# Selective-scan, expert and attention kernel: last C product of a sequence on VectorE, transposes ahead of the gating, normalisation and first tap on ScalarE

## The reference

```
xn = layernorm(x)
# layer 0, a selective scan with 256 channels and 16 states, beside an expert network
hs, gate = split(xn @ in_proj_w.T)
u   = silu(conv1d(hs, conv_w, 4 taps, pad (1, 2)) + conv_b)
dt, Bm, Cm = rmsnorms of the three parts of u @ x_proj_w.T
dt  = softplus(dt @ dt_proj_w.T + dt_proj_b)
h_t = exp(dt_t * A) * h_(t-1) + (dt_t * u_t) * Bm_t        # along the 512 tokens, for 16 states n
y   = sum over n of h[n] * Cm[n] + u * D
y   = y * silu(gate)
x   = x + y @ out_proj_w.T + expert(xn)                    # one of 8 experts per token
# layer 1
xn  = layernorm(x)
x   = x + attention(xn, 16 heads, window +-32) @ Wo + bo + ffn(xn)
```

## Time and profile before

| | |
|---|---|
| median of three runs | 1202.01 us (1197.09 to 1203.52) |
| the profiled execution: its own time | 1201.24 us |
| its span, first to last instruction | 1199.3 us, mean granted TensorE clock 0.922 of 2.4 GHz |
| busy: PE / DVE / ACT / POOL | 925.0 (77%) / 868.6 (72%) / 590.0 (49%) / 434.5 (36%) us |
| chain that ended last, by engine | PE 34%, DVE 26%, issue 16%, POOL 13%, ACT 7% |
| chain, largest lines | DVE hst L709 11%, PE y_bank L1148 10%, POOL hc L1066 7% |
| VectorE gates the sum (L800) at | 243.56, 380.60, 504.64, 628.59, 752.07, 875.71, 999.30, 1109.64 us |

### The profile page before, as it was taken

The page is one execution under the profiler, slowest core; times in us unless marked ns, Lnnn a source line. Parts: engine busy times, 40 slices in busy tenths (PEclk is TensorE's granted clock), DMA queues, the critical chain, the costliest instruction groups (busy, mean ns, idle before and its releaser), DMA issues.

```text
span 1199.3 us, 14581 instructions
## 1 busy us (share of the span) xinstructions
PE 925.0 (77%) x4474; PEld 589.7 (49%) x4474; DVE 868.6 (72%) x1333; ACT 590.0 (49%) x1362; POOL 434.5 (36%) x234
## 2 busy tenths in 40 slices
PE   3553788856887788778879787978787877888786
PEld 2413676724554454445446454545454544455555
DVE  8673544669778977898679868887888778776242
ACT  2142555624654555554555456445635562654442
POOL 3273221343622362237233623363235423533000
PEclk9566999987998999999999999889988999999998
DMA  8163878942321332133223321332223323520000
GB/s 283 48 200 128 247 240 285 238 104 71 83 63 53 97 85 74 49 105 88 73 55 100 92 76 53 87 89 84 60 73 90 78 57 77 105 81 7 10 1 9
DMA packets 79553, 116.77 MB, mean 97 GB/s; under 512 B 4849, under 2 KB 40049, under 8 KB 79345
## 3 DMA queue, kind: packets, MB, share of 16 engines
q1 hardware_dynamic: 73184, 108.99, 32.5%
q0 software_dynamic: 6288, 6.82, 2.5%
HBM read 103.73 MB, written 12.06 MB: 97 GB/s over the span
## 4 chain that ended last, share of the span: by engine, by line
PE 34%; DVE 26%; issue 16%; POOL 13%; ACT 7%; DMA 2%; DVEq 1%; SPq 0%; POOLq 0%; ACTq 0%
DVE hst L709 11%; PE y_bank L1148 10%; POOL hc L1066 7%; PE more L1237 5%; POOL xs_d L1031 3%; DVE dBu L701 3%; POOL x_res L1047 3%; ACT pexp L980 2%; PE work_l L1229 2%; PE work L1167 2%; PE work_l L1223 2%; DVE nmax L823 1%; ACT pT L985 1%; DMA hst<-in_hidden 1%; PE more L1245 1%
## 5 line engine op out<-in xcount | busy, mean ns | idle before, releaser
L1066 POOL TENSOR_TENSOR hc<-hst,bcr 128x1024 f32<-128x1024 f32 x124 | 304.3, 2454 | 600.6 <-DVE dBu L701 547.6
L1148 PE MATMUL y_bank<-hc,pk 128*128 128x512 f32 x512 | 269.1, 652 | 74.7 <-POOL hc L1066 64.1
L709 DVE TENSOR_TENSOR_SCAN hst<-dA,dBu 128x1024 f32<-128x1024 f32 x128 | 291.7, 2279 | 8.0 <-ACT dA L904 5.8
L1148 PEld LDWEIGHTS y_bank<-hc,pk 128*128 128x128 f32 x512 | 98.6, 204 | 186.7 <-POOL hc L1066 86.0
L904 ACT ACTIVATE dA<-dt,neg_a 128x511 f32<-128x511 f32 x256 | 170.6, 726 | 18.8 <-DVE hst L709 16.3
L701 DVE TENSOR_TENSOR dBu<-dtu,bcr 128x1024 f32<-128x1024 f32 x128 | 159.3, 1245 | 12.7
L1237 PE MATMUL more<-vw,pT 96*128 96x99 f32 x1024 | 129.2, 277 | 35.8 <-ACT pT L985 24.5
L1237 PEld LDWEIGHTS more<-vw,pT 96*128 96x128 f32 x1024 | 119.1, 191 | 68.3 <-DVE fsg L843 31.2
L985 ACT COPY pT<-work 96x512 f32<-96x512 f32 x64 | 37.2, 582 | 154.0 <-PE work L1229 154.0
L823 DVE TENSOR_REDUCE nmax<-work 128x4 f32<-128x384 f32 x64 | 35.5, 554 | 62.6 <-PE work L1223 62.6
L980 ACT ACTIVATE pexp<-work_l,nmax 128x96 f32<-128x96 f32 x256 | 66.0, 341 | 5.8 <-DVE nmax L823 5.0
(11 more groups left out here) (293 smaller groups left out, 1459.8 us busy)
## 6 DMA issues: line engine op xcount, KB each, us to landing
bcr<-bc_d SPq DMA_DIRECT2D x128, 512.0 KB, 4.9
qbd<-in_wx SPq DMA_DIRECT2D x8, 578.0 KB, 4.3
attn<-in_wx SPq DMA_DIRECT2D x8, 578.0 KB, 5.0
pT<-in_wx SPq DMA_DIRECT2D x8, 578.0 KB, 5.4
kT<-in_wx SPq DMA_DIRECT2D x8, 578.0 KB, 5.2
vw<-in_wx SPq DMA_DIRECT2D x8, 578.0 KB, 4.9
xs_d<-rbuf POOLq DMA_DIRECT2D x1, 2560.0 KB, 9.8
hst<-in_hidden SPq DMA_DIRECT2D x8, 256.0 KB, 5.4
```

Source lines behind the costliest of these rows:

```text
L709: v.tensor_tensor_scan(hst[n % 2][:].rearrange("p h t -> p (h t)"), dA[n % 2][:].rearrange("p h t -> p (h t)"), dBu[:].rearrange("p h t -> ...
L1066: g_.tensor_tensor(hc[n % 2][:], hst[n % 2][:], bcr[n % RING][:, 1:2, :].to_broadcast([P, NH, L]), ALU.mult).then_inc(s_hc, 1)
L1148: last = t.matmul(y_bank[h][:], ident, hc[n % 2][:, h, :], start=False, stop=(n == N - 1))
```

## The change

It does four things, all in slots 0 to 4 of a turn and at the end of the scan:

1. The C product of the last state, `hc` of n = 15, moves from GpSimd (L1066) to VectorE, right behind the scan of that state and ahead of `dtu`, the last averages and `dBu` of the next sequence. It now waits on VectorE for the product before it and for the sum that read its buffer.
2. Slot 0 begins with the units of a new list `EDGE`: the last sum, then `attnT` (from slot 2), `xnT` (from the middle of slot 0), then the gating (now a unit of its own, `gated`) and `out`. This moves the transposes on TensorE, their copies on ScalarE (L991, L910) ahead of the decay of state 1, and on SyncE the load that follows `xnT`.
3. `ln_b` leaves VectorE: ScalarE computes `xn1` as rstd * x + shift, with a shift of -mean * rstd for which VectorE issues one more small instruction and GpSimd another.
4. `conv0` leaves VectorE: ScalarE computes one tap (that of weight 1, which needs no neighbour) from `bank0` before it copies the projection out, and VectorE adds the taps 0, 2, 3. `bank0` is thus read twice by ScalarE for each of `hs0` and `hs1`.

The core of the diff:

```diff
@@ plan
-PRE_AT = {0: ["xnT"], 1: ["hs0"], 2: ["hs1"], 3: ["conv0", "zg0"], 4: ["conv1", "sg0"], ...
+PRE_AT = {0: ["xnT"], 1: ["hs0"], 2: ["hs1"], 3: ["zg0"], 4: ["conv1", "sg0"], ...
+EDGE = [("attn", "y_end"), ("finish", "attnT"), ("pre", "xnT"), ("attn", "gated"), ("attn", "out")]
...
         if slot == 0:
-            units.append(("attn", "y_end", 0))
-            units += [("attn", name, 0) for name in LAYER1_AT.get(0, [])]
+            units += [(lane, name, 0) for lane, name in EDGE]
@@ VectorE
+                if n == N - 1:
+                    dve.wait_ge(s_h, b * N + N)
+                    dve.wait_ge(s_hc, b * N + N - 1)
+                    dve.wait_ge(s_ys, b * (N + 1) + N - 1)
+                    v.tensor_tensor(hc[n % 2][:], hst[n % 2][:], bcr[n % RING][:, 1:2, :].to_broadcast([P, NH, L]),
+                                    ALU.mult).then_inc(s_hc, 1)
...
+                tap = (1, 0, 2, 3)[k]
                 for h in range(NH):
-                    if k == 0:
+                    if k == 1:
+                        dve.wait_ge(s_tap, b * NH + h + 1)
                         done0(dve, b, f"hs{h}")
-                        before(dve, s_de, b)
-                        v.tensor_scalar(z[0][:, h, :], src, w, half_c[:, NH * KC + h:NH * KC + h + 1],
-                                        ALU.mult, ALU.add).then_inc(s_conv, 1)
...
-                if name == "y_end":
+                if name == "gated":
...
+                    v.tensor_scalar(shift1[:], mv1[:, :, 0], -1.0, None, ALU.mult).then_inc(s_stat1, 1)
-                elif name == "ln_b":
-                    dve.wait_ge(s_rstd1, b + 1)
-                    for j in range(NT):
-                        v.tensor_scalar(xn1[:, j, :], x1r[par][:, j, :], mv1[:, j, 0:1], rstd1[:, j:j + 1],
-                                        ALU.subtract, ALU.mult).then_inc(s_xn1, 1)
@@ ScalarE
+                    s.activation(z[0][:, h, :], bank0[:], ACT.Identity, bias=half_c[:, NH * KC + h:NH * KC + h + 1],
+                                 scale=half_c[:, h * KC + 1:h * KC + 2]).then_inc(s_tap, 1)
                     s.copy(hs[:, h, 1:1 + L], bank0[:]).then_inc(s_free0, 1)
...
                 if name == "ln_b":
+                    act.wait_ge(s_rstd1, b * 2 + 2)
+                    for j in range(NT):
+                        s.activation(xn1[:, j, :], x1r[par][:, j, :], ACT.Identity, bias=shift1[:, j:j + 1],
+                                     scale=rstd1[:, j:j + 1]).then_inc(s_xn1, 1)
@@ GpSimd
-                if n + 1 < N:
-                    pool.wait_ge(s_dBu, b * N + n + 2)
-                else:
-                    pool.wait_ge(s_h, b * N + n + 1)
+                pool.wait_ge(s_dBu, b * N + n + 2)
...
+                        g_.tensor_tensor(shift1[:], shift1[:], rstd1[:], ALU.mult).then_inc(s_rstd1, 1)
```

More of the change, by code:

```diff
@@ L71 @@
 FFN_AT = {12: 0, 16: 1, 20: 2}
-PRE_AT = {0: ["xnT"], 1: ["hs0"], 2: ["hs1"], 3: ["conv0", "zg0"], 4: ["conv1", "sg0"], 5: ["conv2", "zg1"], 6: ["conv3", "sg1"], 8: ["th1"], 9: ["xdbl"], 10: ["ss"], 12: ["xdr"], 13: ["bc"], 15: ["dtT"], 18: ["dtp0"], 19: ["drl0", "dtp1"], 21: ["drl1"], 22: ["de"], 23: ["dw"], 24: ["dln"], 25: ["dt"], 26: ["dtu"], 27: ["start"], 7: ["th0"]}
+PRE_AT = {0: ["xnT"], 1: ["hs0"], 2: ["hs1"], 3: ["zg0"], 4: ["conv1", "sg0"], 5: ["conv2", "zg1"], 6: ["conv3", "sg1"], 8: ["th1"], 9: ["xdbl"], 10: ["ss"], 12: ["xdr"], 13: ["bc"], 15: ["dtT"], 18: ["dtp0"], 19: ["drl0", "dtp1"], 21: ["drl1"], 22: ["de"], 23: ["dw"], 24: ["dln"], 25: ["dt"], 26: ["dtu"], 27: ["start"], 7: ["th0"]}
 LAYER1_AT = {0: ["out"], 1: ["x1"], 2: ["ln_a"], 3: ["ln_b"], 4: ["q", "k"], 5: ["v0", "v1"], 6: ["v2", "v3"]}
 FINISH_AT = {2: ["attnT"], 3: ["fin"], 4: ["y_out"]}
+EDGE = [("attn", "y_end"), ("finish", "attnT"), ("pre", "xnT"), ("attn", "gated"), ("attn", "out")]
 LAG = {"pre": -1, "scan": 0, "attn": 1, "late": 2, "finish": 2}
@@ L97, in plan @@
         units += [(lane, "scores", g) for lane, g in of("scores", slot)]
-        if n is not None:
+        if n is not None and (slot or ("scan", "step") not in EDGE):
             units.append(("scan", "step", n))
@@ L106, in plan @@
             for name in at.get(slot, []):
-                if slot or lane != "attn":
+                if (lane, name) not in EDGE:
                     units.append((lane, name, 0))
@@ L291, in program @@
         rstd1 = sb("rstd1", [P, NT])
+        shift1 = sb("shift1", [P, NT])
         xn1 = sb("xn1", [P, NT, H])
@@ L376, in program @@
         s_conv = sem("conv_steps")
+        s_tap = sem("first_tap_ready")
         s_tg = sem("gate_tanh_ready")
@@ L719, in step @@
                                     ALU.mult).then_inc(s_hc, 1)
+                if n == N - 1:
[4 more added lines that the diff above has]
+                                    ALU.mult).then_inc(s_hc, 1)
             def conv(k, b):
+                tap = (1, 0, 2, 3)[k]
                 for h in range(NH):
[L724 to L726 removed]
+                    if k == 1:
+                        dve.wait_ge(s_tap, b * NH + h + 1)
                         done0(dve, b, f"hs{h}")
[L728 to L734 removed]
+                    else:
+                        dve.wait_ge(s_conv, b * NH * (KC - 1) + (k - 2) * NH + h + 1)
+                    v.scalar_tensor_tensor(z[k % 2][:, h, :], hs[:, h, tap:tap + L],
+                                           half_c[:, h * KC + tap:h * KC + tap + 1], z[(k - 1) % 2][:, h, :],
+                                           ALU.mult, ALU.add).then_inc(s_conv, 1)
             def pre(name, b, par):
@@ L807, in layer1 @@
                     done1(dve, b, "out")
+                    before(dve, s_xn1, b * NT)
                     for j in range(NT):
                         v.bn_stats(stats1[:, j, :], x1r[par][:, j, :]).then_inc(s_stat1, 1)
-                    dve.wait_ge(s_stat1, b * 9 + 4)
+                    dve.wait_ge(s_stat1, b * 10 + 4)
                     v.memset(tick[:], 0.0)
@@ L913, in pre @@
                     full0(act, b, name)
-                    before(act, s_conv, b * NH * KC)
+                    before(act, s_conv, b * NH * (KC - 1))
+                    s.activation(z[0][:, h, :], bank0[:], ACT.Identity, bias=half_c[:, NH * KC + h:NH * KC + h + 1],
+                                 scale=half_c[:, h * KC + 1:h * KC + 2]).then_inc(s_tap, 1)
                     s.copy(hs[:, h, 1:1 + L], bank0[:]).then_inc(s_free0, 1)
@@ L923, in pre @@
                     take0(act, b, name)
-                    act.wait_ge(s_conv, b * NH * KC + (KC - 1) * NH + h + 1)
+                    act.wait_ge(s_conv, b * NH * (KC - 1) + (KC - 2) * NH + h + 1)
                     s.activation(bank0[:], z[1][:, h, :], ACT.Tanh).then_inc(s_full0, 1)
@@ L1072, in body @@
                         early(name, k)
-                    if name == "step" and not (isinstance(b, int) and b == 0 and k < DVE_C):
+                    if name == "step" and k < N - 1 and not (isinstance(b, int) and b == 0 and k < DVE_C):
                         times_c(b, k)
@@ L1083, in body @@
                     elif name == "ln_a":
-                        pool.wait_ge(s_stat1, b * 9 + 9)
+                        pool.wait_ge(s_stat1, b * 10 + 10)
+                        before(pool, s_xn1, b * NT)
                         g_.tensor_tensor(rstd1[:], var1[:], minus_half[:, 0:NT], ALU.pow).then_inc(s_rstd1, 1)
+                        pool.wait_ge(s_rstd1, b * 2 + 1)
+                        g_.tensor_tensor(shift1[:], shift1[:], rstd1[:], ALU.mult).then_inc(s_rstd1, 1)
             iterations(pool, body)
```

7 lines of the change are left out of this document (1 added, 6 removed).

## The result

The changed kernel took 1187.96 us in the median of seven runs (1186.16 to 1192.08), the kernel before 1202.07 on the same chip: ratio 0.9892, 95% interval 0.987 to 0.9914. The forecast of 1189 was met. The profiled execution took 1187.72 us with a span of 1185.9 us, which is 13.4 us less than before; the forecast's sum was 12.7 us. But the sum came out right from terms of which some were wrong by 1 to 4 us in opposite directions, so the profile is worth more here than the total.

A forecast was written before the change was run, and what follows sets the result against it. Neither VectorE nor TensorE is full; what matters is where both stand still, as at the border between turns. Five full turns x 1.75 = 8.8, plus 1.1, 2.5 and 0.3, together 12.7 us: 1189 us, range 1181 to 1198.

The forecast's parts named there:

- The last C product: Border between turns: with the product on VectorE in 1.22 us, the gating starts 2.1 us earlier (1.9 in the worse case).
- The transposes: TensorE at the border: both kinds take 2.0 us, done before the gated halves are there; any delay of `out` is hidden.
- Cost nothing: Border: the moved transposes run from 501.3 to 503.3, before the gated halves at 503.85, so they add no time.
- half-clock rival: Between `hs0` and `hs1`, emptied of `attnT`: TensorE's clock falls before `fin`, `y_out` slips 4.0 us; 1208 us, chance 0.06.
- The chain to `fin`: Gating to `y_out`: `hs1` starts at 514.6 against 516.00, and `y_out` can start 1.9 us earlier, VectorE idle 3.9 us there.
- Some 20 us in all: Sign in the profile after: VectorE waits 3 to 4 us at `y_out` for `fin` in each full turn, this in total.
- The normalisation and the tap: Before `y_out`: 3.19 + 0.99 us leave VectorE, nothing fills their place; ScalarE's normalising, taken as 1.5 us, is hidden.
- The first gated turn: Wait for the expert rows' DMA eats the border's gain; without `y_out` part of the removed work counts: 1.1 us gained.
- Turn 7 and the end: Turn 7, without next input or `hs0`, gains the whole 2.1 plus some tenths: 2.5 us; turn 8 gains 0.3.
- The rival of a quicker TensorE: Border sum and what follows run at full clock, each turn gaining up to 2.6 us: 1183 us, chance 0.2.

The follow-up runs named there:

- x1_hc_only: The kernel before with only the last C product moved to VectorE; order, normalisation and first tap as before: 1188.36 us, ratio 0.9933.
- x9_old_order: The changed kernel with the transposes of attention and of the next input back in their old place: 1187.47 us, ratio 0.9907 to the kernel before.
- x2: The kernel before with only the normalisation and first tap moved to ScalarE; C product and order as before: 1200.23 us, ratio 1.001.
- x10: The changed kernel with only the attention transposes back between the projections; the input's stay ahead of the gating: 1192.11 us, ratio 0.9953 to the kernel before.

## Why the prediction was right, and where it was not

The five full turns, divided at the starts that the timelines give (us in all; in brackets the difference to before):

| | scan of state 15 to gating | gating to scan of state 3 | scan of state 3 to that of state 15 | all |
|---|---|---|---|---|
| before | 46.6 | 106.9 | 464.8 | 618.25 |
| forecast | (-10.5) | (+1.75) | (0) | (-8.8) |
| changed | 40.3 (-6.3) | 109.6 (+2.8) | 463.5 (-1.3) | 613.42 (-4.8) |
| x1_hc_only | 38.3 (-8.3) | 106.8 (-0.1) | 464.2 (-0.6) | 609.31 (-8.9) |
| x9_old_order | 41.5 (-5.1) | 104.8 (-2.1) | 464.1 (-0.7) | 610.41 (-7.8) |

**The last C product: the mechanism right, the size too large.** It took 1.22 us and the `dBu` behind it 1.23, as forecast. But it gave 6.3 us in the five turns where 5 x 2.1 = 10.5 had been taken, and this is the largest part of what is missing. Measured from the scan of state 15, the gating starts 1.7, 1.5, 2.3 and 0.9 us earlier in turns 2, 3, 5 and 6, and in turn 4 not at all (10.17 us against 10.04). Two things stood in the way. The first is in the rows of the changed kernel around the start of turn 3:

```profile
487.83 1.08 PE L1238 MATMUL work<-pk,pexp 128*96 128x128 f32 x4 [1.88 <-ACT pexp L989]
488.71 3.06 PE L1157 MATMUL y_bank<-hc,pk 128*128 128x512 f32 x4
```

```profile
495.03 0.21 DVE L837 RECIPROCAL rden<-more 128x8 f32<-128x8 f32 x1 [0.59 <-PE more L1246]
```

The sum of state 14 runs at half clock, 3.06 us in place of 1.88, so the last attention values come late, and VectorE's reciprocal waits for them. The forecast had let the reciprocal follow `dtu` without a wait. In the twelve traces with this product on VectorE, turn 4 left out, the gating came 7.1 to 7.2 us after the scan in all 27 cases with a fast sum of state 14, and 7.8 to 8.1 us in all 21 with a slow one. The second is in turn 4, before and then after:

```profile
626.02 2.54 PE L1148 MATMUL y_bank<-hc,pk 128*128 128x512 f32 x4 [2.12 <-issue]
```

```profile
619.82 2.86 PE L1157 MATMUL y_bank<-hc,pk 128*128 128x512 f32 x4 [2.04 <-issue]
```

There the sum of state 15 did not wait for the product even before, which GpSimd had ready at 620.99 + 3.17 = 624.16: TensorE stands still for a reason that the profile does not show. It does so at this place in 13 of the 14 traces, for 1.9 to 3.6 us (in x2 the pause of 2.27 us is put down to GpSimd). Turn 4 begins the second pass of the kernel's loop over two turns (`Fori` in `iterations`); that the jump back is the cause is not shown. Then the sum runs at half clock, and the gating waits 2.3 us. x1, which has no slow sum of state 14, got 8.3 us of the 10.5 here, and 2.6 us in turn 7 (110.25 against 112.83), which is the forecast's 2.5.

**The transposes: wrong.** "Cost nothing" is the step that failed. They did not delay `out`, as forecast (they end at 498.36 us and it starts at 498.88, in the rows above). I had weighed whether they delay `out`, and in the rival whether the gap left by `attnT` between the projections lets the clock fall. That gap did not matter (1.43 us, full clock behind it; with `attnT` put back, x10 still had four slow sums). What I did not ask is which pause the other, smaller group had shortened: the one before the state-0 sum grew from at most 1.93 to 2.1 to 2.4 us in four of five turns, and the sum from 1.98 to 3.6 us in three of them. From the gating to the scan of state 3 the changed kernel needs 109.6 us in five turns, with the old order (x9) 104.8. The mechanism of the half-clock rival was at work in another place, and at less than half of its price of 4.0 us.

**The chain to `fin`: right where the clock was full.** `hs1` starts 1.43 us after `hs0` ends (1.6 to 1.8 forecast), ScalarE's four normalising instructions take 1.65 us (1.5 forecast), and `y_out` waits 3.65 us in turns with a full clock (3.9 forecast), 5.2 to 5.4 in the others. "Some 20 us in all" became 36.0: 23.2 in the full turns, since three slow sums add 1.6 each, 2.3 and 2.5 in turns 7 and 8, and the 8.0 of turn 9, which had been there before. That VectorE's busy time would fall by 5 us a turn was a slip: I had left out the product that comes to it. 3.19 + 0.99 + 0.37 of `dBu` less 1.22 and 0.16 makes 3.2, and it fell by 2.8.

**The normalisation and the tap: right, worth next to nothing in full turns.** The stretch from the gating to the scan of state 3 lost 2.0 us in all five turns, both in x2 against before (104.8 against 106.9) and in x9 against x1: 0.4 us of the 4.2 that left VectorE in each turn. In the median x2 shows nothing.

**The first gated turn: mis-sized.** Forecast 1.1, measured 137.35 - 133.25 = 4.1 us, and x2, which has only the normalisation and the tap, has 4.2. Rows of the changed kernel, the answer to 265.61:

```profile
271.09 3.51 DVE L738 SCALAR_TENSOR_TENSOR z<-hs,half_c,z 128x512 f32<-128x512 f32 x2
274.52 0.67 DVE L749 SCALAR_TENSOR_TENSOR sg<-tg,work 128x512 f32<-128x512 f32 x1
275.11 2.27 DVE L711 TENSOR_TENSOR_SCAN hst<-dA,dBu 128x1024 f32<-128x1024 f32 x1
```

No `y_out` stands in the way here, so removed work of VectorE counts, less the 2.1 us that the taps now lose to GpSimd (3.51 in place of 1.40) and plus a wait for `sg0` that is gone: 2.6 us. The other 1.5 us come in the rest of the turn; which of its waits gave them was not traced.

**Turn 7 and the end:** 2.6 (2.5 forecast) and 1.6 (0.3). Turn 7 is 110 to 113 us long; the "120 to 125 us" ahead of the prediction hold for turns 2 to 6 alone. The sum: 0.3 before turn 1, 4.1, 4.8, 2.6, 1.6, together 13.4 us. The 4.0 us missing in the full turns and the 4.7 that came unforeseen elsewhere cancelled: that the sum fits within 0.7 us is luck. So in part is the median: it was met on the first chip, and on the second the gain was half as large. The rival of a quicker TensorE came half true: the sum before the gating ran at full clock in four of five turns (1.90 to 1.98 us, 2.5 to 3.8 before), the sums of states 0 and 14 more often at half.
